# A vision-transformer tower on one core: the first tile's inputs in thirds, its roots on two engines, q and k ahead of v

## What is computed

```python
h = patches @ W.T + b, with the class token in front, + pos_embedding
h = h + attn_block(_layernorm(h))      # two layer norms in a row at its start:
    xn = layer_norm(x, ln1_w, ln1_b)
    q, k, v = (xn @ w.T + b).reshape(B, N, H, D) for each
    q, k = elu(q) + 1, elu(k) + 1
    kv = einsum('bhnd,bhne->bnde', k, v)
    attn = einsum('bhnd,bnde->bhne', q, kv) / (q . sum of k over the heads)
    x = x + attn @ o_w.T + o_b
    x = x + gelu(layer_norm(x, ln2_w, ln2_b) @ fc_w.T + fc_b) @ proj_w.T + proj_b
h = h + ffn(_layernorm(h))             # 16 experts, top-C tokens of each, + a shared one
```

## Time and profile before

| | us |
|---|---|
| median of 3 runs | 484.55 (484.29 to 484.92) |
| the profiled execution | 485.78 |
| its span in the trace | 484.0 |
| TensorE busy | 436.4 (90%) |
| VectorE busy | 349.8 (72%) |
| ScalarE busy | 253.7 (52%) |
| GpSimd busy | 209.5 (43%) |

### The profile page before, as it was taken

How to read it: one execution, slowest core, us unless ns; L and a number is a source line. 1 busy time by engine, 2 the same in 40 slices (tenths; PEclk the granted TensorE clock), 3 DMA queues, 4 the chain that set the end, 5 groups by cost and what they waited for, 6 DMA issues and landing times.

```text
span 484.0 us, 10715 instructions
## 1 busy us (share of the span) xinstructions
PE 436.4 (90%) x3999; PEld 383.5 (79%) x3999; DVE 349.8 (72%) x634; ACT 253.7 (52%) x639; POOL 209.5 (43%) x233
## 2 busy tenths in 40 slices
PE   7899989888798999988896989899999999999990
PEld 3568768767776877877785869799999999999980
DVE  1099998998998999211698897888777777777620
ACT  1575477687586764445441014555566656655520
POOL 1355442966865353232000144464644744444432
PEclk9999999999999999999799999999999999999995
DMA  6723490000000000000000029787889888888321
GB/s 244 260 77 100 171 428 5 13 12 0 12 12 1 12 12 12 1 14 22 8 0 0 2 76 375 278 310 280 319 309 333 318 309 322 316 316 295 101 28 14
DMA packets 17351, 69.15 MB, mean 143 GB/s; under 512 B 4338, under 2 KB 10399, under 8 KB 12834
## 3 DMA queue, kind: packets, MB, share of 16 engines
q1 hardware_dynamic: 12130, 61.96, 34.4%
q0 software_dynamic: 4608, 5.41, 5.5%
q10 hardware_dynamic: 576, 1.29, 0.7%
HBM read 63.32 MB, written 5.33 MB: 142 GB/s over the span
## 4 chain that ended last, share of the span: by engine, by line
PE 48%; DVE 10%; ACT 4%; DMA 2%; issue 2%; POOL 1%; ACTq 0%; DVEq 0%; POOLq 0%
PE bank L1474 18%; PE bank L1485 12%; PE bank L1239 4%; DVE scratch L1017 3%; PE bank L1268 3%; DMA wex_s<-in_wex 2%; PE bank L1253 2%; PE bank L1226 2%; DVE wproj_s L1000 2%; PE bank L1496 1%; DVE late L1069 1%; PE bank L1381 1%; PE bank L1452 1%; PE bank L1194 1%; PE bank L1166 1%
## 5 line engine op out<-in xcount | busy, mean ns | idle before, releaser
L530 POOL DMA_INDIRECT out_rows<-scratch,slot_s x32 | 54.1, 1690 | 80.0 <-DMA out_rows<-scratch,slot_s 60.0
L1485 PE MATMUL bank<-scratch,wex_s 128*128 128x148 f32 x512 | 77.7, 295 | 0.5 <-DVE scratch L1109 0.5
L519 POOL DMA_INDIRECT xg<-token_rows,slot_g x32 | 44.8, 1400 | 70.9 <-DVE slot_g L1082 62.0
L1485 PEld LDWEIGHTS bank<-scratch,wex_s 128*128 128x128 f32 x512 | 67.6, 190 | 1.0 <-DVE scratch L1109 1.0
L802 ACT ACTIVATE scratch<-bank 128x296 f32<-128x296 f32 x64 | 26.6, 416 | 67.7 <-PE bank L1474 67.0
L1474 PE MATMUL bank<-scratch,wfc_s 128*128 128x148 f16 x512 | 52.6, 227 | 0.3 <-DVE wproj_s L1000 0.3
L1474 PE MATMUL bank<-scratch,wsh_s 128*128 128x148 f16 x512 | 52.7, 227 | 0.0
L1474 PE MATMUL bank<-scratch,wproj_s 128*128 128x148 f16 x256 | 50.6, 227 | 0.0
L860 DVE TENSOR_TENSOR scratch<-qk 128x2048 f32<-128x2048 f32 x20 | 46.7, 2351 | 5.1 <-PE bank L1253 4.8
L1000 DVE SCALAR_TENSOR_TENSOR wproj_s<-wex_s,wfc_s 128x512 f16<-128x512 f32 x64 | 40.4, 683 | 11.6 <-ACT wfc_s L785 11.6
L1109 DVE SCALAR_TENSOR_TENSOR scratch<-bank,scratch 128x296 f32<-128x296 f32 x64 | 29.4, 460 | 26.5 <-ACT scratch L802 26.2
(11 more groups left out here) (171 smaller groups left out, 939.6 us busy)
## 6 DMA issues: line engine op xcount, KB each, us to landing
wex_s<-in_wex SPq DMA_DIRECT2D x16, 2048.0 KB
wex_s<-in_wex SPq DMA_DIRECT2D x16, 1024.0 KB, 8.3
patch_s<-in_patches SPq DMA_DIRECT2D x10, 384.0 KB
token_rows<-y_s SPq DMA_DIRECT2D x10, 128.0 KB, 1.7
out_rows<-h_all SPq DMA_DIRECT2D x5, 256.0 KB
wex_s<-in_wfc SPq DMA_DIRECT2D x1, 1024.0 KB, 7.1
wproj_s<-in_wproj SPq DMA_DIRECT2D x1, 1024.0 KB, 9.2
wsh_s<-in_wsh SPq DMA_DIRECT2D x1, 1024.0 KB, 6.0
```

Source lines behind the costliest of these rows:

```text
L519: gp.indirect_dma_start(xg[b][:], None, rows, bass.IndirectOffsetOnAxis(slot_g[b][:], 0))\
L530: gp.indirect_dma_start(out, bass.IndirectOffsetOnAxis(slot_s[b][:], 0), eo[b], None, compute_op=ALU.add).then_inc(scattered, 16)
L1485: last = pe.matmul(ps_down[k][:, 0:C], wex_s[s.par][:, lo:lo + P], hexT[:, m, :], start=(m == 0), stop=(m == MC - 1))
```

## The change

The first tile's weights and patches come in thirds (two of the six chunks each), each third half on SyncE's queue and half on ScalarE's; the second tile's patches come in two halves. Of the constants only the identity (`ident`) is loaded early, the rest later on SyncE's queue. `embed_first` waits for each third by itself and takes the position and bias product last. Six matmuls stand where 14 stood, and three where twice four stood around the transposition of tile 0. For tile 0, VectorE does the small steps of the two norms (`first_shift`) and GpSimd only the two powers. ScalarE makes `xnT` of tile 0 before it copies tile 1, and copies v after exp; TensorE projects q and k of tile 0 before v.

```diff
--- before.py
+++ after.py
@@ -50,7 +50,8 @@
 WEX = WGU + MC * D
 SCRATCH = max(H * D, (2 * KC + 4 + MC + KC + 2 * KC) * C + 4 * D)
 EPS = 1e-5
-WARM = 14
+WARM = 6
+CHUNK = TKC // 3
 
 
 
@@ -270,6 +271,8 @@
 
         w_in = {n: sem(f"in_{n}") for n in ("bias", "consts", "tok", "qkv", "o", "fc", "proj", "moe")}
         patch_in = [sem(f"patch_in{b}") for b in range(2)]
+        first_in = [sem(f"first_in{c}") for c in range(4)]
+        rest_in, var_made, root_made = sem("rest_in"), sem("var_made"), sem("root_made")
         gu_in = [sem(f"gu_in{b}") for b in range(2)]
         dn_in = [sem(f"dn_in{b}") for b in range(2)]
         y_out = [sem(f"y_out{b}") for b in range(2)]
@@ -346,13 +349,19 @@
                 sp.dma_start(patch_s[s.par][:], patches[s.n]).then_inc(patch_in[s.par], 16)
                 sp.dma_start(sel_s[s.par][:], sel[s.n]).then_inc(patch_in[s.par], 16)
 
-            sp.dma_start(wtok_s[:], wtok).then_inc(w_in["tok"], 16)
-            load_patch(Step(0, 0))
+            third = lambda c: slice(c * CHUNK, (c + 1) * CHUNK)
+            half = TKC // 2
+            sp.dma_start(wtok_s[:, third(0), :], wtok[:, third(0), :]).then_inc(first_in[0], 16)
+            sp.dma_start(patch_s[0][:, third(1), :], patches[0, :, third(1), :]).then_inc(first_in[1], 16)
+            sp.dma_start(wtok_s[:, third(2), :], wtok[:, third(2), :]).then_inc(first_in[2], 16)
             sp.dma_start(base_s[:], base).then_inc(w_in["tok"], 16)
+            sp.dma_start(sel_s[0][:], sel[0]).then_inc(patch_in[0], 16)
+            sp.dma_start(patch_s[1][:, 0:half, :], patches[1, :, 0:half, :]).then_inc(patch_in[1], 16)
+            sp.dma_start(sel_s[1][:], sel[1]).then_inc(patch_in[1], 16)
 
             sp.wait_ge(bias_made, 5)
             sp.dma_start(parts.rearrange("n (p j) -> p n j", p=P), bpart[:]).then_inc(bias_out, 16)
-            load_patch(Step(0, 1))
+            sp.dma_start(kst[:, K_TRI:KCOLS], consts[:, K_TRI:KCOLS]).then_inc(rest_in, 16)
             sp.wait_ge(ones_made, 1)
             sp.wait_ge(bias_out, 16)
             for n, q in enumerate(PARTS):
@@ -488,7 +497,11 @@
                 base = count - n
                 return lambda k: base + k
 
-            norm_a(Step(0, 0), after(5))
+            gp.wait_ge(var_made, 1)
+            gp.tensor_tensor(rstd[:, 0:1], tmp[:, 0:1], nhalf[:], ALU.pow).then_inc(root_made, 1)
+            gp.wait_ge(var_made, 2)
+            gp.tensor_tensor(rstd[:, 3:4], tmp[:, 5:6], nhalf[:], ALU.pow).then_inc(a_rstd, 1)
+
             norm_a(Step(0, 1), after(5))
             norm_a(Step(0, 2), after(5))
             for t in range(TILES + 3):
@@ -562,7 +575,12 @@
                 act.activation(warm[:, 1:2], warm[:, 0:1], ACT.Exp)
 
             act.dma_start(braw[:], bias).then_inc(w_in["bias"], 16)
-            act.dma_start(kst[:], consts).then_inc(w_in["consts"], 16)
+            for c in range(3):
+                dst, src = (wtok_s, wtok) if c == 1 else (patch_s[0], patches[0])
+                act.dma_start(dst[:, c * CHUNK:(c + 1) * CHUNK, :], src[:, c * CHUNK:(c + 1) * CHUNK, :])\
+                   .then_inc(patch_in[0] if c == 2 else first_in[c], 16)
+            act.dma_start(patch_s[1][:, TKC // 2:, :], patches[1, :, TKC // 2:, :]).then_inc(first_in[3], 16)
+            act.dma_start(ident, consts[:, K_ID:K_TRI]).then_inc(w_in["consts"], 16)
             act.dma_start(colc[:], cols).then_inc(w_in["consts"], 16)
             act.dma_start(wqkv_s[:], wqkv).then_inc(w_in["qkv"], 16)
             act.wait_ge(ones_made, 1)
@@ -678,11 +696,11 @@
             copy_h(Step(0, 0))
             norm_a(Step(0, 0))
             scale_xh(Step(0, 0))
+            turn_xn(Step(0, 0))
             copy_h(Step(0, 1))
-            turn_xn(Step(0, 0))
-            copy_v(Step(0, 0))
             negate_qk(Step(0, 0))
             exp_qk(Step(0, 0))
+            copy_v(Step(0, 0))
             norm_a(Step(0, 1))
             scale_xh(Step(0, 1))
             copy_h(Step(0, 2))
@@ -844,7 +862,20 @@
                     step += 1
                     ve.wait_ge(bias_made, step)
                 src = brest
-            ve.wait_ge(w_in["consts"], 32)
+            def first_shift():
+
+                one = lambda a, n: a[:, n:n + 1]
+                squares = spread[:, 0, 0:1]
+                ve.wait_ge(a_stats, 1)
+                ve.tensor_scalar(one(tmp, 0), squares, 1 / D, EPS, ALU.mult, ALU.add).then_inc(var_made, 1)
+                ve.wait_ge(root_made, 1)
+                ve.scalar_tensor_tensor(one(tmp, 4), one(rstd, 0), one(rstd, 0), squares, ALU.mult, ALU.mult).then_inc(v_passed, 1)
+                ve.tensor_tensor(one(shift, 0), one(rstd, 0), less[:, 0, 0:1], ALU.mult).then_inc(a_shift, 1)
+                ve.wait_ge(v_passed, 1)
+                ve.tensor_scalar(one(tmp, 5), one(tmp, 4), 1 / D, EPS, ALU.mult, ALU.add).then_inc(var_made, 1)
+
+            first_shift()
+            ve.wait_ge(rest_in, 16)
             ve.tensor_copy(iota_b[:], kst[:, K_IOTA:K_IOTA + HC]).then_inc(v_passed, 1)
             ve.tensor_copy(same_b[:], kst[:, K_SAME:K_SAME + P]).then_inc(v_passed, 1)
             ve.tensor_copy(tri_b[:], kst[:, K_TRI:K_TRI + P]).then_inc(casts_made, 1)
@@ -1175,10 +1206,23 @@
                 pe.wait_ge(patch_in[s.par], s.half * 32 + 32)
                 if t >= 2:
                     pe.wait_ge(h_copied, t - 1 if t < TILES - 1 else t)
+                if t == 1:
+                    pe.wait_ge(first_in[3], 16)
                 pe.matmul(ps_tok(t)[:, 0:D], sel_s[s.par][:], base_s[:], start=True, stop=False)
                 for k in range(TKC):
                     last = pe.matmul(ps_tok(t)[:, 0:D], patch_s[s.par][:, k, :], wtok_s[:, k, :], start=False, stop=(k == TKC - 1))
                 last.then_inc(tok_done, 1)
+
+            def embed_first():
+
+                for k in range(TKC):
+                    if k % CHUNK == 0:
+                        pe.wait_ge(first_in[k // CHUNK], 16 if k // CHUNK == 2 else 32)
+                    if k == 2 * CHUNK:
+                        pe.wait_ge(patch_in[0], 32)
+                    pe.matmul(ps_tok(0)[:, 0:D], patch_s[0][:, k, :], wtok_s[:, k, :], start=(k == 0), stop=False)
+                pe.wait_ge(w_in["tok"], 16)
+                pe.matmul(ps_tok(0)[:, 0:D], sel_s[0][:], base_s[:], start=False, stop=True).then_inc(tok_done, 1)
 
             def turn_xh(s):
                 pe.wait_ge(xh_made, s.times(1, 1))
@@ -1291,17 +1335,16 @@
 
             pe.wait_ge(ones_made, 1)
             keep_busy(WARM)
-            pe.wait_ge(w_in["tok"], 32)
-            embed(0)
+            embed_first()
             embed(1)
             pe.wait_ge(w_in["consts"], 32)
-            keep_busy(4)
             turn_xh(Step(0, 0))
-            keep_busy(4)
+            keep_busy(3)
             pe.wait_ge(bias_in, 16 * len(PARTS))
             pe.wait_ge(w_in["qkv"], 16)
+            pe.wait_ge(xnT_made, 1)
+            project_qk(Step(0, 0))
             project_v(Step(0, 0))
-            project_qk(Step(0, 0))
             embed(2)
             turn_xh(Step(0, 1))
             embed(3)
```

## The result

The changed kernel takes 481.01 us (median of 5 runs, 480.28 to 484.21) against 484.55 (484.11 to 485.28, 5 runs) before: a ratio of 0.993, 95% interval 0.9903 to 0.9957. It is faster, by 3.5 us; 480.7 was predicted.

The account below looks back on a forecast made before the run. TensorE, late through the first turns, was taken to decide: 2.49 + 0.38 + 0.80 = 3.7 us, plus 0.2 from VectorE's lead, 3.9 in all; from 484.55 to a median of 480.7 us, range 479.3 to 482.9.

Parts of the forecast that it names:

- TensorE's frontier: Start of tile 2's embedding, from which TensorE runs without a gap; 3.7 us earlier, near 18.0, and this moves the end.
- Rival C: VectorE decides, as each turn's attention waits for its products; 4.7 to 5 us reach the end, 479.6 us; chance 0.12.
- the new wait of turn 1: In turn 1 VectorE waits for TensorE's sums, a new wait of up to 1 us.
- rival D: GpSimd and VectorE meet in another phase, stretching GpSimd's one-column steps; slower than before, 486.3 us; chance 0.05.
- Embedding of tile 0: At the start, tile 0 is embedded 2.49 us earlier (11.41 to 8.92); 1.9 with half the load rate.
- its clock rises at 6.3 us as before: During tile 0's embedding TensorE's clock rises at 6.3 us; 1.58 us at half speed before it, end at 8.92.
- rival B: TensorE's clock rises late, at 10.4 us; tile 0 done at 11.0, 2.1 us of gain lost, 482.8 us; chance 0.14.
- the thirds are in at about 3.5, 4.5 and 5.4 us: Tile 0's weights and patches land then, near the full 407 GB/s, with a spare microsecond on each third.
- Roots, 0.38 us: Tile 0's norm steps shared by VectorE and GpSimd take 2.56 us instead of 2.94; bounds 0.03 to 0.8 saved.
- ScalarE's order, 0.80 us: `xnT` of tile 0 no longer waits behind tile 1's copy and squares on ScalarE: 0.80 us saved.
- Matmuls dropped in the middle at no cost: Dropping the four ahead of tile 0's transposition costs nothing; three instead of four behind it end before `xnT` is ready.
- The moved transfers at no cost: Constants go ahead of the bias rows, which are in by about 12 us and first needed at 15.0; no wait.

Follow-up runs that it names:

- the repetition: The changed kernel itself, unchanged, timed and profiled a second time: 482.43 us (10 runs), ratio 0.9941 to the kernel before.
- roots and orders alone: Kernel before with only shared norm steps, xnT ahead of tile 1's copy, q and k before v: 485.15 us, 1.0001; with the tower-end stands filled 482.14, 0.9947.
- filled stands: Ten matmuls without use added around the tower's last transposition of y (four ahead, six behind); on the changed kernel 479.05 us, 0.9876; measured again 479.58, 0.9911.
- the old roots: The changed kernel with all small steps of tile 0's two norms back on GpSimd: 482.94 us, ratio 0.9944 to the kernel before.
- the loading alone: Kernel before with only loading in thirds, embedding by thirds and six warm-up matmuls: 483.69 us, 0.9956; with the tower-end stands filled 481.87, 0.9943.

## Why the prediction came out right, point by point

The time was right (480.7 for 481.01) and the mechanism was right. That the sum came out is in part luck: the embedding was put too high, the roots too low, and a gain of 0.28 us in the middle of the tower stood in no term.

**TensorE's frontier decides, and the offset is carried.** Right. Turn 3's step stands 55.83 to 55.85 us behind the embedding of tile 2 in the profiles with q and k first, however late that embedding is (17.63 to 20.59), and 55.92 to 55.94 with v first. Rival C falls with it: VectorE's 0.97 us of lead reached it as 0.09 us, where 0.2 was put into the sum, and the rest became the new wait of turn 1. That wait was predicted, but at up to 1 us, and it is 3.51: the lead did put GpSimd and VectorE in another phase, as rival D had it, only to VectorE's good (2.29 us for the product that took 4.23), and the wait took all of it back. The loss that rival D feared isn't seen.

Behind turn 3 the offset grows once. From that step to the last transposition of the tower it is 148.62 to 148.68 us in all ten profiles with the thirds, and 148.91 and 148.97 in the two with the old loading and no second dip. Nearly all of it comes in one place: ScalarE's `x` of turn 7 starts 0.12 us behind the end of GpSimd's shift (148.57 + 0.19) in the profile after and 0.40 behind it (149.83 + 0.19) in the one before. The two rows, the kernel before first (timelines of 144 to 152 us):

```profile
150.42 0.60 ACT L600 ACTIVATE x<-x_all,shift,rstd 128x256 f32<-128x256 f32 x1 [3.42 <-POOL shift L439]
148.88 0.60 ACT L618 ACTIVATE x<-x_all,shift,rstd 128x256 f32<-128x256 f32 x1 [3.14 <-POOL shift L448]
```

All four profiles with the old loading have these 0.28 us and none of the ten with the thirds. Nothing in the prediction foresaw them, and what causes them stays open.

**Embedding of tile 0, 2.49 us.** Mis-sized: it is worth 1.9 on the mean, and varies (the prediction's own lower value, at half the rate, was 1.9). Eight profiles with the thirds and six matmuls ahead copy tile 0 at 11.93, 9.51, 9.62, 8.98, 10.15, 8.99, 9.57 and 9.73 us, mean 9.81. Four with the old loading copy it at 11.52, 11.73, 11.89 and 11.72, mean 11.72. The best two have what was predicted. Two assumptions failed in the others.

First, "its clock rises at 6.3 us as before". The clock of the profile after was low past 10.9 us, later than rival B's 10.4, and in the repetition it was up before 5.7. So rival B happens: in one of the eight profiles, in which the late clock and the wait together cost 2.95 us against the best (11.93 to 8.98). The mean of the other seven is 9.51. The Trainium skill (TensorE: Matmul & The Clock Gate, Part 1: The HAM clock gate (the "warmup" mystery)) says that the start of the upper clock differs from run to run; the traces agree, with a far wider spread than its half microsecond; its matmuls run without a gap, while here a wait for a transfer stands among them. The old loading isn't free of this, but hides it: with roots and orders alone and filled stands, the 14 matmuls took 5.88 us, nearly all at the lower clock, and still ended before the last transfer:

```profile
2.16 5.88 PE L1310 MATMUL bank<-ones_b 128*128 128x512 bf16 x14 [2.16 <-POOL warm L427]
8.20 0.70 PE L1198 MATMUL bank<-base_s,sel_s 39*128 39x256 f32 x2 [0.16 <-DMA base_s<-in_base]
```

The change puts useful work where the clock is uncertain, so it is worth more in some executions than in others.

Second, "the thirds are in at about 3.5, 4.5 and 5.4 us and position and selection at 5.6, whichever queue they are on". The second third came later in all eight: at 5.7 to 6.1 us in three, in time for TensorE, and at 6.85 to 7.49 in five. The step that failed is the order. In the profile after 1.56 MB had moved by 7.2 us, and in that of the old roots 1.28 by 5.7 us, while the first two thirds are 0.79: what was issued behind the second third moved beside it. In order, the rate of the profile after would have brought it at about 4.6 us (an estimate: 0.30 MB by 3 us, then 299 GB/s to 7.2 us). The lower rate then adds to the delay. All transfers, 3 to 8 us, in the profile after and in that of the old roots, as in the earlier trace rows:

```profile
DMA packets 1405, 1.53 MB, mean 307 GB/s; under 512 B 315, under 2 KB 1123, under 8 KB 1405
```

```profile
DMA packets 1619, 1.95 MB, mean 391 GB/s; under 512 B 390, under 2 KB 1273, under 8 KB 1619
```

Before, it was 407 GB/s in 856 packets; the four profiles with the old loading have 384 to 407. With nearly twice the packets the rate lies at 307 to 391 GB/s, and changes by execution; in the five where the third came late it was 307 to 340, in the three others 373 and more. That small pieces cause it fits, but no run loaded in thirds with larger ones. The Trainium skill (DMA: Bandwidth & Descriptors, Issuing engines are not separate DMA queues) says that transfers issued by several engines share the same DMA engines; the traces agree: the transfers of both queues moved side by side (1.56 MB before the first two thirds, 0.79 MB of it, were complete), and together they never brought more than the 407 GB/s of before.

**Roots, 0.38 us.** Mis-sized: 0.86 from the squares to `xh` (2.94 to 2.08), and 0.91 by the way from copy to tile 2 against the old roots. The failed step is "other hops I put between, at 0.1 to 0.12", and 0.23 to GpSimd: measured were 0.04, 0.08, 0.04, 0.08 and 0.14 us, 0.38 together where the sum had 0.80, in part below the 0.08 with which the upper bound of 0.8 was worked out, so that the term fell outside its bounds; and VectorE's steps on one column took 0.15 us for 0.17.

**ScalarE's order, 0.80 us.** Right: 0.81. In the profile after, the transposition and what follows `xnT` stand at

```profile
16.18 0.41 PE L1197 MATMUL bank<-kst,xh 128*128 128x128 f32 x2 [1.07 <-ACT xh L638]
17.58 0.38 PE L1201 MATMUL bank<-bias_s,ones_b 65*128 65x512 bf16 x1 [0.34 <-ACT xnT L642]
```

so `xnT` (16.63) starts 0.45 us behind the start of the transposition, and started 1.26 behind it before (16.54 to 17.80).

**Matmuls dropped in the middle at no cost.** Nearly right: it cost 0.09 us. With them the transposition starts 0.05 us behind the end of `xh` (15.98 + 0.51 = 16.49 to 16.54 before, and 0.05 or 0.06 in all six profiles that keep them), without them 0.14 (16.04 to 16.18, and 0.14 or 0.15 in all eight without). The reason given, "the earlier stands of 0.78 and 0.89 us didn't lower the clock", is no rule: in the loading alone with filled stands, stands of 0.97 and 0.89 us did, for 1.6 us.

**The sum.** From copy to tile 2 it is 0.86 + 0.81 - 0.09 = 1.58 us for the 1.18 predicted, and 1.55 measured. The whole is 1.9 + 1.55 + 0.09 + 0.28 = 3.8 us for the 3.9 predicted, and 3.5, 3.4 and 3.6 were measured in three comparisons (484.55 to 481.01, 485.81 to 482.43, 483.16 to 479.58); the interval of the first alone is 2.1 to 4.7.

**The moved transfers at no cost.** Right: the bias rows are issued at 10.1 to 11.4 us and never waited for, and the casts hide behind the shift.

**"By 152 us every row stands 3.7 to 4.0 us earlier."** Wrong for the profile shown, which stands 1.2 us earlier at 76 us and 1.6 at the end; right for an execution with the early clock: the repetition stands 3.67 us earlier at 74.00 (77.67 before), and 3.98 at ScalarE's `x` of turn 7 (146.44 for 150.42). Executions of the one changed kernel differ by 3.9 us (480.28 to 484.21), more than the change is worth.

**Not foreseen.** The dip at the tower's end, 0 to 3.1 us, which both kernels have. It isn't a part of the change. With it filled, roots and orders alone show a gain of 1.0 us where they showed none; that this dip had hidden it is possible, not shown; the second dip, of 145 to 165 us, could have done it as well. Filled, it gives 0.34% on the kernel before, and with the change 479.05 and 479.58 us, ratios of 0.9876 and 0.9911: the fastest version here, with 479.44 for the one that has ten matmuls ahead as well. What decides in which execution the clock falls stays open; no run here told it.

## What to carry to other kernels

Find the one instruction from which the engine that is late through the next stage runs without a gap, and count only what moves that: VectorE's lead of 1 us, grown to 2.9 by turn 1, was worth 0.09. Transfers issued together move side by side, so count all of them and not only the one that is waited for first. Work that is pulled forward into the first microseconds meets a clock and a load rate that vary by execution, so take its gain as a range, and read two or three profiles before a step of a microsecond is believed. Where the busiest engine stands for a microsecond twice in a row, look at the clock behind it, and fill the stands if it falls.

## What the runs showed of the hardware

- The granted clock fell behind stands of only 0.88 and 1.34 us, at one place of these programs, in seven of eight profiles, at a cost of 1.5 or 3.1 us; with matmuls in the stands in none of six. At another place, stands of 0.97 and 0.89 us had the clock fall behind them in one profile and 0.98 and 0.89 left it up in another.
- At the start the time of the rise differed by more than 5 us between two executions of one program. The clock column reads 1.00 in the first windows although the matmuls of 512 columns stand 0.43 us apart: there the level has to be read from the spacing.
- A semaphore's hop took 0.04 us from ScalarE to VectorE and from GpSimd to VectorE, 0.08 from VectorE to GpSimd, and 0.14 from GpSimd to ScalarE (14.82 + 0.57 = 15.39 to 15.53). A chain of small steps over two engines was 0.9 us shorter than on GpSimd alone, with three hops more (2.08 and 2.98 us).
- Loads in pieces of 1 and 2 KB ran at 307 to 391 GB/s from 3 to 8 us (ten profiles), those of 3 and 6 KB at 384 to 407 (four). A transfer of 256 KB issued at 1.66 us landed 4.0 to 5.8 us later, with 1.28 to 1.8 MB moved by then.
- One VectorE product of 128x2048 numbers took 4.23 us beside GpSimd's conversion of 128x1024 and 2.29 where that came later.
